# Half of a value projection issued one slot earlier, in a kernel of two attention blocks on Trainium2

## What is computed

```
for i in range(6):
    x = attn_layer(shift_tokens(x), Wqkv[i], q_scale[i], k_scale[i], Wo[i]) + x
    x = ffn_layer(shift_tokens(x), ln_g[i], ..., W2[i], b2[i]) + x
# attn_layer: q, k, v = split(x @ Wqkv)        128 -> 3 * 1024, 16 heads of 64
#   q, k = l2norm(q) * qs, l2norm(k) * ksc, then rotary tables
#   out  = local attention: a window of 32 queries sees its own 32 keys and the 32 before
#   return out @ Wo                            1024 -> 128
```

## Time and profile before

| | us |
|---|---|
| time, median of 3 runs (lowest to highest) | 3899.53 (3894.57 to 3904.09) |
| the profiled execution: its own time | 3896.07 |
| its span, from the first to the last instruction | 3894.3 |
| PE busy | 3698.3 (95%) |
| DVE busy | 3006.1 (77%) |
| POOL busy | 2602.0 (67%) |
| ACT busy | 2289.8 (59%) |
| granted TensorE clock, mean, share of full speed | 0.983 |

### The profile page before, as it was taken

One profiled execution on the slowest core, in us unless ns is written; L12 is line 12 of the kernel. 1 busy time (PEld: TensorE's weight loads), 2 busy tenths in 40 slices (PEclk: granted clock), 3 DMA queues, 4 the chain that ended last, 5 costly groups with the idle time before them and its releaser, 6 DMA issues.

```text
span 3894.3 us, 163005 instructions
## 1 busy us (share of the span) xinstructions
PE 3698.3 (95%) x67712; PEld 2834.8 (73%) x67712; DVE 3006.1 (77%) x5061; ACT 2289.8 (59%) x4270; POOL 2602.0 (67%) x3029
## 2 busy tenths in 40 slices
PE   5999979999999999999999999999999999999998
PEld 3555547778768878677787678887688886777876
DVE  7666658888678888678887788886788886888876
ACT  3555546666546666456666466665466664566652
POOL 4545448888548888368887288885488873688870
PEclk8999989999999999999999999999999999999999
DMA  1000002222212222122222022222122221222220
GB/s 45 4 6 4 6 27 71 57 61 61 59 32 61 58 59 58 42 50 61 60 59 56 28 68 59 58 61 59 32 61 58 61 57 40 54 57 59 61 52 23
DMA packets 136307, 189.03 MB, mean 49 GB/s; under 512 B 38006, under 2 KB 58484, under 8 KB 135412
## 3 DMA queue, kind: packets, MB, share of 16 engines
q1 hardware_dynamic: 135540, 178.23, 17.7%
HBM read 22.67 MB, written 2.10 MB: 6 GB/s over the span
## 4 chain that ended last, share of the span: by engine, by line
PE 74%; issue 4%; POOL 4%; DVE 3%; ACT 1%; DMA 0%; POOLq 0%; SPq 0%; DVEq 0%; ACTq 0%
PE PS L1270 18%; PE PS L1418 9%; PE PS L1256 9%; PE PS L1294 8%; PE PS L1258 8%; PE PS L1257 8%; PE PS L1280 8%; PE PS L1477 3%; PE PS L1412 1%; PE PS L1455 1%; POOL t L1182 1%; PE PS L1448 1%; POOL t L1187 1%; PE PS L1443 1%; DVE t L1766 0%
## 5 line engine op out<-in xcount | busy, mean ns | idle before, releaser
L1182 POOL TENSOR_TENSOR t<-t 128x1024 f32<-128x1024 f32 x384 | 908.9, 2371 | 319.7 <-DVE t L1767 318.7
L1187 POOL TENSOR_TENSOR t<-t,rn 128x1024 f32<-128x1024 f32 x384 | 724.1, 1907 | 29.9 <-POOL rn L150 27.3
L1766 DVE TENSOR_TENSOR t<-PS,rope 128x512 f32<-128x512 f32 x768 | 523.8, 682 | 30.3 <-ACT sq L1578 28.4
L1256 PE MATMUL PS<-w_hi,xh 128*128 128x512 f32 x1152 | 512.9, 445 | 22.0 <-DVE xl L1063 11.3
L1767 DVE TENSOR_TENSOR t<-PS,rope 128x512 f32<-128x512 f32 x768 | 523.0, 681 | 0.0
L1578 ACT ACTIVATE sq<-PS 128x512 f32<-128x512 f32 x768 | 455.0, 594 | 34.1 <-PE PS L1258 18.8
L1270 PE MATMUL PS<-constants,t 128*128 128x128 f32 x3072 | 456.2, 281 | 18.9 <-POOL t L1187 13.1
L1258 PE MATMUL PS<-w_lo,xh 128*128 128x512 f32 x1152 | 459.6, 399 | 0.0
L1257 PE MATMUL PS<-w_hi,xl 128*128 128x512 f32 x1152 | 459.0, 398 | 0.0
L1773 DVE TENSOR_REDUCE ss<-sq 128x16 f32<-128x1024 f32 x384 | 448.4, 1209 | 0.0
L1418 PE MATMUL PS<-oT,w_out 128*128 128x128 f32 x3072 | 394.9, 281 | 1.0 <-issue 0.5
(11 more groups left out here) (167 smaller groups left out, 7760.2 us busy)
## 6 DMA issues: line engine op xcount, KB each, us to landing
vs<-va SPq DMA_DIRECT2D x768, 130.0 KB
vs<-va SPq DMA_DIRECT2D x768, 65.0 KB
t<-in_L_ffn_Wqkv SPq DMA_DIRECT2D x18, 512.0 KB, 4.4
w_out<-in_L_ffn_Wo SPq DMA_DIRECT2D x6, 512.0 KB, 3.8
a_normed<-in_L_attn_x SPq DMA_DIRECT2D x8, 256.0 KB, 6.4
a_xo<-in_L_attn_x SPq DMA_DIRECT2D x8, 256.0 KB, 2.9
out<-total SPq DMA_DIRECT2D x8, 256.0 KB, 3.5
w_raw<-in_L_ffn_W SPq DMA_DIRECT2D x6, 341.0 KB
```

What stands on the lines that cost most here:

```text
L1182: pool.tensor_tensor(mine[:, i, :], mine[:, i, :], t2[:, i, :], ALU.add).then_inc(done, 1)
L1187: pool.tensor_tensor(h, h, bc(rn[:, H * i:H * (i + 1)], 2, HB), ALU.mult).then_inc(done, 1)
L1256: pe.matmul(out, hi, w_hi, start=True, stop=False)
L1766: dve.tensor_tensor(o1, src, bc(rope[:, 2 * i, t, :], 1, 8), ALU.mult)
```

## The change

In the slot of tile T, V0 of tile T is no longer issued at the start. It is issued in the slot of tile T-1, between the output projection and the second half of the scores. Slot (0, 1), which has no full slot ahead of it, keeps V0 at its start, and the last slot of a layer, (7, 3), issues none for a next tile. Q1 is issued right after Q0, and with that the two halves of the transposes of the weights stand next to each other. The instructions of the other engines are the same and stand in the same order.

```
+        def after(s, t):
+            return (s, t + 1) if t + 1 < TPS else (s + 1, 0)
...
-                if project_new:
-                    if t % 2 == 0:
-                        pe.wait_ge(xl_made, 2 * halves(lay, s, t // 2) + 2)
+                if (s, t) == (0, 1):
                     pe.wait_ge(rq_made, at(T, 1, 2, 2))
                     project(2, 0, 7, t, v_mm)
-                    if s == 0 and t == 1:
-                        pe.wait_ge(rk_made, at(T, 1, 2, 2))
+                    pe.wait_ge(rk_made, at(T, 1, 2, 2))
                 pe.wait_ge(attn_done, at(T, 3, 1, 1))
                 if project_new:
                     project(1, 0, 4, t, k_mm)
                     project(1, 1, 5, t, k_mm)
                     pe.wait_ge(v_made, at(T, 1, 2, 2))
                     project(0, 0, 6, t, q_mm)
+                    pe.wait_ge(v_made, at(T, 0, 2, 1))
+                    project(0, 1, 7, t, q_mm)
...
                 if mix:
                     turn_weights(0)
-                if project_new:
-                    pe.wait_ge(v_made, at(T, 0, 2, 1))
-                    project(0, 1, 7, t, q_mm)
-                if mix:
                     turn_weights(1)
...
+                if project_new and (s, t) != (B - 1, TPS - 1):
+                    s_next, t_next = after(s, t)
+                    if t_next % 2 == 0:
+                        pe.wait_ge(xl_made, 2 * halves(lay, s_next, t_next // 2) + 2)
+                    pe.wait_ge(rq_made, at(T, 0, 2, 2))
+                    project(2, 0, 7, t_next, v_mm)
                 if score:
                     score_half(1).then_inc(s_mm, 1)
```

## The result

The changed kernel takes 3960.58 us (median of 6 runs, 3957.23 to 3967.46), the kernel before 3900.97 us (6 runs, 3894.57 to 3904.09). The ratio is 1.0157, with a 95% interval of 1.0144 to 1.017: about 60 us slower. The forecast was slower, 3998 us in a range of 3950 to 4035. The sign and the mechanism held. The size was two thirds above what came, and the measured time lies nearer to the case *more comes back* (3953 us, given 10%) than to the forecast itself.

A forecast was written before the change was run, and what follows sets the result against it. Each slot was a ring: scores' end to V1, PE and DVE level at 6.4 us, then PE alone, 7.8 us. 168 x (0.79 - 0.05) = 124 us, less 25, gave 3995 us profiled, 3998 us forecast; range 3950 to 4035.

The forecast's parts named there:

- more comes back: Rival: all PE stalls in scores and mixing disappear and V0 costs 0.70 us; 55 us slower, 3953 us; 10%.
- Two chains of equal length in the first stretch: From the scores' end to V1, PE and DVE both need 6.4 us, so removing V0 there leaves DVE's time.
- V0 lengthens the second stretch by its full price: From V1 to the next scores' end PE runs alone, 7.8 us; V0 adds 0.79 us a slot.
- The slack of 0.05 us: Between the scores' end and V1, taking V0 out gains only 0.05 us a slot, bounds 0 and 0.11.
- What comes back: PE's stalls on late instructions in scores and mixing shrink, gaining 25 us, between nothing and about 54 us.
- Two slots a layer free: In (0, 2) and (7, 3) existing PE waits absorb the later scores' end, leaving 28 slots a layer, 168.
- Q1's move free: Ahead of the mixing, Q1's move costs nothing; PE still reaches V1 some 0.2 us before DVE frees the bank.
- The sum: Over 168 slots, 0.79 less 0.05 us each is 124 us; less 25 us of stalls, 99 us slower.
- The rigid 6.13 us: Sign: DVE's distance from its maxima to its last rope of Q0 stays at 6.13 us.
- V1's distance from the rope: Sign: PE's weight load for V1 follows the end of DVE's rope by 0.06 us in nearly all slots.
- PE alone: Rival: only PE's work bounds the kernel, so nothing changes and the time is 3898 us; 3%.
- ACT in DVE's place: Rival: bare PE-ACT hand-overs at the weight transposes start mixing 0.15 us too late; 25 us more, 4022 us; 14%.

The follow-up runs named there:

- the short rope: DVE's rope of Q0 cut to 64 of 512 columns: on the changed kernel 3936.24 us, ratio 1.0092; on the kernel before 3900.58 us, ratio 0.9997.
- the later copies: SP's copies va to vs wait for the scores' end: on the kernel before 3895.16 us, ratio 0.9986; on the changed kernel 3957.04 us, ratio 1.0171.

## Why the prediction was right, and where its size was off

- *Two chains of equal length in the first stretch: right.* The rope's end holds V1 in nearly every slot now (0.054 us in the mean), a cut of DVE's chain in the changed kernel gains 0.15 us a slot, not 0.7, and a cut in the kernel before gains nothing. A projection put back into the free stretch is almost free.
- *V0 lengthens the second stretch by its full price: right, the price was too high.* The shortest V1 to maxima grew by 8.266 - 7.567 = 0.70 us, not by the 0.79 us that I took from Q1. From the start of the output projection it takes 1.81 us to V0 (698.02 to 699.83), where it took 1.98 us to the scores (medians of 168 slots; the 2.06 of the earlier trace rows is a long one), and V0 itself takes 0.88: the net is 0.70. V0's weight load starts beside the last matmuls of the output projection (699.80, the last of them starting at 699.80 too), which I take for the reason; no run tests it. This is 168 x 0.09 = 15 us of the forecast's excess.
- *The slack of 0.05 us: right,* 6.245 - 6.191 = 0.054.
- *What comes back: right in kind, too small.* The mean over the shortest of the second stretch fell from 0.405 to 0.172 us, 0.23 us a slot and 39 us in all, where I took 25 between 0 and 54. The scores' stalls went from 5.7 + 18.0 to 1.0 + 2.5 us, those of the mixing's second half from 32.1 to 14.8 us. I had thought that the mixing would keep most of its own, since it gains only a wait of 0.2 us. That it lost half of them stays unexplained, all the more as it did not with V0 ahead of both halves of the scores, at the same wait.
- *Two slots a layer free, Q1's move free: right.* PE is ready for V1 0.19 us before DVE has freed the bank, by the short rope and by V1's waits. I had estimated 0.2. But only the exponentials hold PE, not the copy that I had named as the later of the two.
- *The sum:* 168 x (0.70 - 0.054) = 109 us, less 39 is 70 us in the slots, against 67.5 in the windows; outside them 3 us less. The terms that were off are a pair of sizes, 15 us in the price of V0 and 14 us in the stalls, and both pointed the same way. The rest of the distance from 3998 to 3960.58 us is 5 us between this sum and the growth of the span, and the 3.5 us that I added for a median above the profiled execution, which the changed kernel does not show (3960.96 us profiled).
- *The signs.* The rigid 6.13 us and V1's distance from the rope came as said, and DVE's wait grew by 0.60 us, near the 0.7. A slot of 14.8 or 14.9 us did not (14.63), nor did 0.6 us of idle PE time (0.42), a steady busy time (0.16 us more a slot), or a wait ahead of the mixing.
- *The rivals.* PE alone: refuted by the 60 us, and by 130 us of extra matmuls that cost 15. ACT in DVE's place: it is the next limit, not the present one. *More comes back* was the better forecast, since two of its terms were near the truth. The share of 10% that I gave it was low for a case that differed only in two unknown prices.

No version that computes the whole result beats the kernel before by more than the later copies do (0.14%, with an interval from 0.04% to 0.24%). That the stalls are late instructions is shown by their place and by the packets. What remains open is why PE must wait at some borders of a block and not at others: spacing and DMA traffic both move it, and neither accounts for all of it.

## What to carry to other kernels

In a software pipeline, write the loop down as a ring and ask of each stretch which engines run it side by side. Work taken out of a stretch that two engines share gains nothing when both need the same time, and put into a stretch that one engine runs alone it costs its full price, even though no engine gets more to do. A kernel whose PE is busy 95% of the time can thus be made slower without giving PE any work. A page that shows no wait at such a place may mean two chains that meet, so compare the end of the one with the start of the other before moving anything.

## What the runs showed of the hardware

A run of 64 small matmuls with their weight loads takes 0.79 us, and PE stalls inside such runs with no semaphore to wait for, in the second half of the mixing by up to 0.98 us in the kernel before and 1.75 us with V1 behind the mixing. The stalls stand at every 256th instruction and end 1.22 to 1.61 us after a 16 KB packet of the instruction queue has ended. The Trainium skill (Runtime: NRT & Kernel Launch, Instruction fetch mechanics) describes blocks of 256 instructions of which the next is fetched while one runs. The trace agrees on the size; two runs of 128 instructions each hold as many as such a block. Spacing them by 0.7 us of other work changed the stalls of the second from 81.6 us to 32.1 us (V1 between the halves of the mixing) and from 18.0 to 2.5 us (V0 between the halves of the scores). The page calls the cost mostly hidden; in the kernel before it was (32.1 + 18.0 + 5.7) / 180 = 0.31 us of a 14.2 us slot.
